# Trainium2 decoder kernel: order of slots laid anew with 429 fillers at 55 places, and a ternary weight's sums taken on TensorE by products with ones

## The reference

```
delta = 0.7 * mean(|w|)
mask  = |w| > delta
alpha = sum(|w| * mask) / max(sum(mask), 1)
wq    = alpha * sign(w) * mask
```

## Time and profile before

| | |
|---|---|
| median of three executions | 1320.36 us |
| the profiled execution | 1321.37 us |
| its span, first to last instruction | 1319.7 us |
| PE, DVE, ACT, POOL busy, share of the span | 89%, 69%, 52%, 18% |
| mean granted clock of TensorE | 0.960 |
| fillers on PE | 300, 80.3 us busy |

### The profile page before, as it was taken

How to read it: one execution, slowest core, us unless ns; L and a number is a source line. 1 busy time by engine, 2 the same in 40 slices (tenths; PEclk the granted TensorE clock), 3 DMA queues, 4 the chain that set the end, 5 groups by cost and what they waited for, 6 DMA issues and landing times. The chain is left out here.

```text
span 1319.7 us, 27471 instructions
## 1 busy us (share of the span) xinstructions
PE 1170.9 (89%) x10598; PEld 790.7 (60%) x10598; DVE 911.6 (69%) x2410; ACT 689.6 (52%) x1307; POOL 234.0 (18%) x337
## 2 busy tenths in 40 slices
PE   7769999999999999998997899889778898799885
PEld 4446767776777676775554666545555465556542
DVE  5463383375499968798976698866788766756466
ACT  2234454555554565445565546657427555377524
POOL 3320121112110130012201013010120112301122
PEclk8889999999999999999998999989999999899987
DMA  7001111211112100210000010000000000000000
GB/s 287 16 1 48 49 34 32 65 41 41 33 49 78 35 17 25 72 33 17 1 1 2 2 34 9 1 1 2 2 1 1 2 1 2 1 2 2 1 1 33
DMA packets 23288, 35.59 MB, mean 27 GB/s; under 512 B 4584, under 2 KB 12920, under 8 KB 22904
## 3 DMA queue, kind: packets, MB, share of 16 engines
q1 hardware_dynamic: 23160, 33.83, 8.1%
HBM read 32.77 MB, written 1.05 MB: 26 GB/s over the span
## 5 line engine op out<-in xcount | busy, mean ns | idle before, releaser
L2238 DVE TENSOR_REDUCE arena<-banks 128x4 f32<-128x1024 f32 x128 | 150.6, 1218 | 74.6 <-PE banks L2066 73.9
L1354 PEld LDWEIGHTS banks<-WE,arena 128*128 128x128 f32 x1536 | 180.0, 192 | 24.5 <-issue 22.6
L1354 PE MATMUL banks<-WE,arena 128*128 128x128 f32 x1536 | 182.7, 276 | 0.1
L1398 ACT ACTIVATE arena<-banks,BC 128x512 f32<-128x512 f32 x192 | 129.5, 691 | 99.9 <-PE banks L1338 99.6
L1338 PE MATMUL banks<-XT,WE 128*128 128x512 f32 x384 | 179.7, 604 | 0.0
L2218 ACT ACTIVATE arena<-banks 128x1024 f32<-128x1024 f32 x128 | 124.1, 1022 | 71.2 <-PE banks L2090 71.2
L1438 DVE SCALAR_TENSOR_TENSOR R<-banks,arena,R 128x128 f32<-128x128 f32 x256 | 72.0, 344 | 107.0 <-PE banks L1354 106.4
L613 ACT COPY arena<-banks 128x512 f32<-128x512 f32 x100 | 57.7, 589 | 120.4 <-PE banks L608 36.7
L2319 POOL TENSOR_TENSOR arena<-arena 128x256 f32<-128x256 f32 x56 | 43.6, 778 | 381.6 <-ACT arena L2200 381.6
L1338 PEld LDWEIGHTS banks<-XT,WE 128*128 128x128 f32 x384 | 69.6, 193 | 66.7 <-issue 65.7
L1900 DVE TENSOR_TENSOR arena<-arena 128x512 f32<-128x512 f32 x144 | 100.5, 698 | 3.9
(11 more groups left out here) (329 smaller groups left out, 2121.3 us busy)
## 6 DMA issues: line engine op xcount, KB each, us to landing
WE<-in_weights SPq DMA_DIRECT2D x64, 256.0 KB, 2.9
WE<-in_weights SPq DMA_DIRECT2D x64, 128.0 KB, 2.2
WS<-in_weights SPq DMA_DIRECT2D x1, 2368.0 KB, 14.3
RW<-in_rows SPq DMA_DIRECT2D x1, 1032.0 KB
XALL<-in_x SPq DMA_DIRECT2D x4, 256.0 KB, 10.9
out_dram<-arena SPq DMA_DIRECT2D x4, 256.0 KB, 2.3
WS<-in_weights SPq DMA_DIRECT2D x1, 900.0 KB, 9.0
WS<-in_weights SPq DMA_DIRECT2D x1, 645.0 KB, 9.1
```

The lines of the kernel that those rows point to most:

```text
L1354: ins = PE.matmul(v[:, tile(t)], self.HT[:, e % 2, j, tile(t)], self.W[:, (8 * i + e) % RING, 1, j], start=j == 0, stop=j == self.J - 1)
L1398: A.activation(self.HT[:, e % 2, j], psum.view(f"{self.L}.h{i}.{e}.{j}"), ACT.Relu, bias=bcol(self.p + "_b1", e * self.J + j))\
L2238: V.tensor_reduce(big.mx[:, 2 * pair:2 * pair + 2], v, AX.X, ALU.max, negate=True).then_inc(dve.read(f"big.m{i}.{n}.{pair}"), 1)
```

## The change

Six things are changed.

1. `TURNS` is another order of the same 504 slots. The first 23 slots are as before, and so are the last 77 but for two swaps of neighbours (chunk 3's `big` 20 and 22 now come after chunk 2's `x3` 5 and 7).
2. `FILLERS` has 429 products at 55 places instead of 300 at 45.
3. The two `partition_all_reduce` on POOL go. In their place PE multiplies a 128 x 128 tile of ones by the 128 x 8 tile `tern_sums`, once in slot 3 and once in slot 7 of chunk 0's `x0`, and DVE reads the sums from PSUM.
4. `tern_scale_dve` moves on DVE from slot 7 of chunk 0's `x0` to slot 8, ahead of that stage's end sum.
5. Two memsets (the ones, and zeros in `tern_sums`) are added to DVE's setup, ahead of its wait for `small_loaded`.
6. In `big`, `scores` and `values` take their banks ahead of their other waits, and get a place for fillers. `FILLERS` uses two of these, `big.o0.15` and `big.o3.15`, with three products each.

```diff
-HEADS_MADE = 26
+HEADS_MADE = 28
 FILLERS = {
-    "in.xT0": 12, "ret.s0.0": 12, "ret.yT0": 12, "ret.y.out0": 3, "ret.xT0": 12, "ret.yT1": 2, "x0.pv1.1": 3,
-    "x0.xT2": 4, "spm.xT0": 3, "moe1.xT1": 5, "one.xT2": 2, "moe1.xT2": 11, "lora.zT0": 3, "x2.pn1.1": 3,
-    "cos.xT3": 11, "lora.xT0": 9, "big.hT0.0": 12, "one.xT3": 7, "moe1.xT3": 2, "x2.xT2": 12, "x3.pn0.1": 3,
-    "x3.o.out0": 4, "lora.zT2": 4, "lora.xT2": 6, "big.xT1": 12, "big.hT2.0": 5, "spm.xT3": 4, "x2.pv3.1": 2,
-    "x2.pn3.1": 3, "x2.o.out3": 3, "x2.xT3": 7, "big.xT2": 12, "lora.zT3": 3, "lora.xT3": 12, "big.hT3.0": 3,
-    "x3.pn2.1": 3, "x3.o.out2": 3, "big.xT3": 27, "x3.hT3.0": 7, "x3.hT3.1": 2, "x3.pv3.1": 3, "x3.pn3.1": 3,
-    "x3.oT3": 4, "x3.o.out3": 3, "last.max": 22,
+    "in.xT0": 17, "ret.s0.0": 23, "ret.yT0": 30, "ret.y.out0": 3, "ret.xT0": 25, "x0.pn0.1": 3, "ret.yT1": 12,
+    "x0.pv1.1": 1, "x0.pn1.1": 3, "ret.yT2": 1, "cos.xT2": 7, "x2.hT0.0": 1, "moe1.xT2": 11, "x2.pv1.1": 6,
+    "x2.pn1.1": 2, "cos.xT3": 7, "x2.oT1": 3, "lora.xT0": 7, "x2.xT1": 2, "one.xT3": 11, "big.hT0.0": 1,
+    "big.hT0.1": 2, "big.o0.15": 3, "x2.pv2.1": 1, "x2.pn2.1": 3, "moe1.xT3": 1, "x2.xT2": 19, "big.hT1.0": 1,
+    "x3.pv0.1": 5, "big.hT1.1": 2, "x3.o.out0": 5, "big.xT1": 30, "big.hT2.0": 6, "big.hT2.1": 2, "spm.xT3": 4,
+    "x2.hT3.1": 2, "x2.pv3.1": 6, "x2.pn3.1": 3, "x2.o.out3": 3, "x2.xT3": 8, "big.xT2": 19, "lora.zT3": 6,
+    "lora.xT3": 22, "big.hT3.0": 4, "big.o3.15": 3, "x3.pv2.1": 7, "x3.o.out2": 3, "big.xT3": 30, "x3.hT3.0": 7,
+    "x3.hT3.1": 4, "x3.pv3.1": 7, "x3.pn3.1": 3, "x3.oT3": 4, "x3.o.out3": 3, "last.max": 25,
 }
 TURNS = (
-    "00000000000000010010110101010100111100010101012012010202101121021012020210211202010210120121230102303310212302"
-    "03013133023120320120102100132123102103010021020213002012121020131223121232132012203201023231023021010320120211"
-    "23033101333131211331213320120321313202110023103212132033212311321310323100001000320200200000300103230223013123"
-    "02302203213023202032023023202133100111030101311111011112113211212112311122122232312232213231221323121322113232"
-    "3323332332233233232323323333333333333333332322332223233333333333"
+    "00000000000000010010110010010011110010100101010120101222101211201012020221011202102021201020321203331021023323"
+    "02120210203133102130302130302313032001031103010201312131002132012310201132121013213212320122021030202012012011"
+    "31312131323212102113212321020130302132031302301232131223211013013130231010300303202023000023010100002023200312"
+    "02310220323023202022303232302311013010130011011011311112113123121213112131122122222222132312213213121322113232"
+    "3323332332233233232323323333333333333333332232323223233333333333"
 )
@@ setup_dve
+            nc.vector.memset(R[:, CHUNKS - 1, 3], 1.0).then_inc(heads_made, 1)
+            nc.vector.memset(tern_sums[:], 0.0).then_inc(heads_made, 1)
@@ the ternary weight
+        def tern_total_pe(pe):
+            v = psum.take(pe, "tern.total")
+            pe.wait_ge(heads_made, HEADS_MADE)
+            pe.wait_ge(sig("tern.rows"), 1)
+            PE.matmul(v[:, 0:8], tern_ones, tern_sums[:], start=True, stop=True).then_inc(psum.filled("tern.total"), 1)
+        def tern_totals_pe(pe):
+            v = psum.take(pe, "tern.totals")
+            pe.wait_ge(sig("tern.parts"), 1)
+            PE.matmul(v[:, 0:8], tern_ones, tern_sums[:], start=True, stop=True).then_inc(psum.filled("tern.totals"), 1)
@@ tern_parts_dve
-            dve.eng.wait_ge(sig("tern.total"), 1)
+            dve.eng.wait_ge(*psum.made("tern.total"))
@@ tern_scale_dve
-            dve.eng.wait_ge(sig("tern.totals"), 1)
+            dve.eng.wait_ge(*psum.made("tern.totals"))
@@ Cross.pe, slot 3
                 self.shifts_pe(pe, i, 1)
+                if L == "x0" and i == 0:
+                    tern_total_pe(pe)
@@ Cross.pe, slot 7
                     fold_product_pe(pe)
+                    tern_totals_pe(pe)
@@ Cross.dve
+                yield
                 if L == "x0" and i == 0:
                     tern_scale_dve(dve)
-                yield
@@ Cross.pool
-                    G.partition_all_reduce(tern_total, tern_row, P, bass.bass_isa.ReduceOp.add)\
-                        .then_inc(pool.flag("tern.total"), 1)
...
-                    G.partition_all_reduce(tern_totals, tern_row_sums, P, bass.bass_isa.ReduceOp.add)\
-                        .then_inc(pool.flag("tern.totals"), 1)
@@ scores(n) of big
+                v = [psum.take(pe, f"big.e{i}.{n}.{pair}", 2) for pair in range(2)]
+                keep_awake(pe, f"big.e{i}.{n}", v[0][:, 0])
                 pe.wait_ge(*psum.copied(f"big.hT{i}.{n}"))
-                v = [psum.take(pe, f"big.e{i}.{n}.{pair}", 2) for pair in range(2)]
@@ values(n) of big
+                v = psum.take(pe, f"big.o{i}.{n}")
+                keep_awake(pe, f"big.o{i}.{n}", v)
                 for pair in range(2):
                     pe.wait_ge(*psum.copied(f"big.e{i}.{n}.{pair}"))
                 pe.wait_ge(*psum.copied(f"big.v{i}.{n}"))
-                v = psum.take(pe, f"big.o{i}.{n}")
```

More of the change, by code:

```diff
@@ L847, in ret_pool @@
             yield from end_slots_pool(pool, "ret", i)
-        tern_row, tern_total, tern_delta, tern_ndelta = (tern_sums[:, k:k + 1] for k in range(4))
-        tern_row_sums, tern_totals = tern_sums[:, 4:6], tern_sums[:, 6:8]
-        tern, tern_neg, tern_w = (R[:, CHUNKS - 1, k] for k in range(3))
+        tern_row, tern_count, tern_delta, tern_ndelta = (tern_sums[:, k:k + 1] for k in range(4))
+        tern_row_sums = tern_sums[:, 4:6]
+        tern, tern_neg, tern_w, tern_ones = (R[:, CHUNKS - 1, k] for k in range(4))
+        def tern_total_pe(pe):
[7 more added lines that the diff above has]
+            PE.matmul(v[:, 0:8], tern_ones, tern_sums[:], start=True, stop=True).then_inc(psum.filled("tern.totals"), 1)
         def tern_rows_dve(dve):
@@ L865, in tern_parts_dve @@
             w = W("L3_ffn_weight")
-            dve.eng.wait_ge(sig("tern.total"), 1)
-            V.tensor_scalar(tern_delta, tern_total, 1.0 / (D * D), 0.7, ALU.mult, ALU.mult).then_inc(dve.step(), 1)
+            dve.eng.wait_ge(*psum.made("tern.total"))
+            V.tensor_scalar(tern_delta, psum.view("tern.total")[:, 0:1], 1.0 / (D * D), 0.7, ALU.mult,
+                            ALU.mult).then_inc(dve.read("tern.total"), 1)
             dve.eng.wait_ge(*dve.own())
@@ L882, in tern_scale_dve @@
         def tern_scale_dve(dve):
[L884 to L885 removed]
+            totals = psum.view("tern.totals")
+            dve.eng.wait_ge(*psum.made("tern.totals"))
+            V.tensor_scalar(tern_count, totals[:, 5:6], 1.0, None, ALU.max).then_inc(dve.step(), 1)
             dve.eng.wait_ge(*dve.own())
[L887 removed]
+            V.reciprocal(tern_delta, tern_count).then_inc(dve.step(), 1)
             dve.eng.wait_ge(*dve.own())
[L889 removed]
+            V.tensor_tensor(tern_delta, tern_delta, totals[:, 4:5], ALU.mult).then_inc(dve.read("tern.totals"), 1)
         plain = XB[:, slot(CHUNKS - 1), 0:3]
```

7 lines of the change are left out of this document (removed).

## The result

The kernel after takes **1301.35 us** (median of 4 executions, 1297.75 to 1303.53) against 1321.0 us for the kernel before beside it (4, 1319.93 to 1323.68): ratio 0.9846, 95% interval 0.9816 to 0.9875. The profiled execution took 1302.88 us, span 1301.2, which is 18.5 us less than the profiled one of before. The forecast was 1312.6 in a range of 1301 to 1322, with faster by over 0.2% at 0.72: the sign was right and the range just held, but the forecast of 7.8 us less was under half of the 19.7 that came.

What follows compares the result with a forecast made beforehand. PE was taken to bound 104 to 594 us, with all engines waiting in turn elsewhere. Opening -8.4, start fillers +3.6, full stretch 0, sorts -3, end 0 gave -7.8: 1312.6 us against the median, range 1301 to 1322.

Steps and rivals of the forecast that it cites:

- Same work on PE in another order: Full stretch, 104 to 594 us: reordering the same PE work changes 0 us, bounds -4 and +4.
- nothing but less work on PE shortens it: Full stretch: PE busy 483.7 of 490 us at 2.4 GHz, so only less PE work could shorten it.
- The stretch from 594 us has 8.5 us without PE; -1: Stretch just ahead of chunk 0's `big`: of 8.5 us without PE, the new order wins 1 us.
- The opening: End of chunk 0's `x0`: all-reduces on POOL hold everybody; removing them and reordering gives -8.4 us, bounds -13 and -3.
- The products "hidden": Chunk 0's `x0`: two products of ones on PE, 0.3 us each, at most 0.7, hidden since PE waits around them.
- What gives back: Opening: `ret` 10 and 11 moved into the full stretch, +1.5 us; ten more fillers and a wait, +2.6 us.
- Fillers of chunk 0's `ret`: Start of kernel: added fillers cost 1.1 + 2.4 + 1.2 + 0.4, clock returns 1.5; +3.6 us, bounds 0 and +10.
- Taking banks ahead of other waits: In `big`: taking banks earlier alters nothing, since all the waits must end anyway; zero.
- The sorts: Beside `big`: a sort between two slots costs about 4.6 us; -4 around chunk 0's `big`, +2 around chunk 1's.
- The tail of the sorts is worth more: Rival, chance 0.22: in three stretches from 594 us on, 12 us without PE go instead of 3; 1304 us.
- Absorbed: Rival, chance 0.17: DVE or the new fillers swallow the opening's gain before 594 us; 1318 to 1320 us.
- half absorbed: Rival, 0.07 of the 0.17: weight loads tell PE's fullness, half the opening's 4.8 us is lost; 1318 us.

Runs made afterwards that it cites:

- e5: Kernel after with slots 84 to 253 in the order of before: 1314.12 us, ratio 0.9939.
- e11: Kernel before with the ternary sums on PE and the new order and fillers in slots 15 to 83 alone: 1311.84 us, ratio 0.9931.
- e15: Kernel after without the steps of five of chunk 2's sort slots (sort left unfinished): 1296.66 us, ratio 0.9811.
- e1: Kernel before with items 3 to 6 only (ternary sums on PE, memsets, earlier banks), order and fillers of before: 1321.75 us, ratio 0.9995.
- e2: Kernel before with the new order and fillers only (without the six of item 6), sums still on POOL: 1305.61 us, ratio 0.9869.
- e9: Kernel after with slots 0 to 83 and their fillers as before, ternary sums staying on PE: 1305.05 us, ratio 0.9872.
- e3: Kernel after with the 300 fillers at 45 places of before: 1310.33 us, ratio 0.9889.
- e8: Kernel after with 12 fillers at each of four places in chunk 0's `ret`, instead of 17, 23, 30 and 25: 1298.65 us, ratio 0.9813.
- e13: Kernel before without the steps of seven of chunk 1's sort slots (sort left unfinished): 1324.29 us, ratio 1.0019.
- e16: Kernel after without the steps of seven of chunk 1's sort slots (sort left unfinished): 1306.82 us, ratio 0.9885.
- e6: Kernel after with slots 254 to 326 in the order of before, fillers of after: 1319.12 us, ratio 0.9989.
- e10: Kernel after with slots 254 to 326 and the fillers there as before: 1320.79 us, ratio 0.9994.
- e17: Kernel before with chunk 0's `lora` 2 and 3 moved later and without three fillers at `lora.zT0`: 1325.00 us, ratio 1.0024.

## Why the prediction was right or wrong

- **"Same work on PE in another order ... I take 0, bounds -4 and +4": the step that failed**, and with it "nothing but less work on PE shortens it". Slots 84 to 253 measured -5.2. I read 483.7 us busy of 490 as work. Beside the 6.3 us idle, the busy time held 14 fillers, and groups of transposes that a wait breaks in two count 0.88 us as busy where a whole one counts 0.60. Of the gain 1.8 us were idle PE and 3.4 counted as busy.
- **"The stretch from 594 us has 8.5 us without PE; -1": failed too.** It measured -4.8: 3.5 of idle PE (8.6 to 5.1) and 1.3 of busy. e5 shows that the gain depends on the order ahead of it.
- **The opening: right in what holds it, by luck in the size.** POOL's `norm_mean` begins where forecast, and e11 shows the gain at the end of the kernel. Slots 15 to 38 gave 12.5 us where -10.5 + 1.5 - 2.0 = -11.0 was forecast. But idle PE fell by 7.9, less than the 10.5 of that term, and the clock gave 4.6, more than its 2.0. In other executions of these slots the clock gave less; e15 took 47.3 us. The 6.95 us for the sums and 3.5 for the order were misdivided as well: in idle time e1 and e2 show 3.1 and 4.1 for them alone.
- **The products "hidden": wrong for the old order, nearly right for the new.** I asked whose semaphore they wait for and not who waits for their bank: 3.1 to 3.3 us in e1 and e9. With the new opening the wait that e11 shows for that reader is 0.6 us.
- **What gives back: a little too much.** For the ten fillers at `ret.yT1` I took +2.6; slots 39 to 83 show +1.7 or +1.8 in every kernel with the new order and fillers and the sums on PE. e3, with 2 fillers there, takes 113.8 us and not less than after's 113.3, so they cover a wait.
- **Fillers of chunk 0's `ret`, +3.6: right in sum** (+3.8; e8 gives 2.7 us back between medians). The 17 fillers end at 7.73 and the scores start at 17.51, 0.7 and 1.0 us ahead of what I wrote.
- **Taking banks ahead of other waits, "so zero": wrong.** A `big` slot without other waits takes 5.26 us with item 6 and 5.15 without it.
- **The sorts: the price near, the saving not there.** Forecast -4 around chunk 0's `big`; measured -1.1, with no less idle PE (14.4 and 15.1), in slots that vary by 4 us with the clock. Forecast +2 around chunk 1's, measured +1.2, which is no more certain. The 3.3 us wait is at its place.
- **The rivals.** "The tail of the sorts is worth more", 1304, is nearest in number and wrong in mechanism. "Absorbed" and "half absorbed" fall by e11: 10.3 us at slot 84 are 10.3 at the end. The half-absorbed case was the one that the Trainium skill's rule favours (Trainium Kernel Development and Optimization, Performance Expectations: matmul busy time is a bad metric for how close a kernel is to the roofline, weight loads a good one). With weight loads busy for 350.7 of 490 us this stretch still passed a gain on whole, so as a sign of what bounds the stretch the rule would have misled here. The Trainium skill's GPSIMD Engine Reference (opening) calls POOL the correct choice for reductions over partitions. That would have misled too: e2, with the sums on POOL and the new order, reaches slot 84 at 219.1 us, the kernels with the sums on PE and the new opening at 204.4 to 215.4.
- **The marks of "wrong"** (start of `moe0` at 94 or later, over 10 us of idle PE up to 590, over 152 or under 140 between the two `big` 9) were all kept clear: 89.73, under 5, 146.5. They watched for a loss alone; none would have shown a gain that I had not counted.

**Still open:** which neighbours in slots 84 to 288 make the 10 us. Shown is that it isn't chunk 1's sorts (e13, e16), that with the old order in either half it is gone (e5, e6), with that half's own fillers too where it was tried (e10), and that one chain given cover only moves the wait (e17). That the waits at stage ends make about half of the 5.2 us is read from the traces and fits e5; no run isolates it. What item 6 costs the whole kernel is open too.
